# Routed experts with the weights standing still: a ring of six expert tiles, gate and up left turned, biases as columns

## What is computed

```python
logits = x @ router_weight.T + router_bias
top_val, top_idx = jax.lax.top_k(logits, TOP_K)
router_scores = zeros.at[rows, top_idx].set(softmax(top_val))
gate_up = einsum('th,ehd->etd', x, gate_up_proj) + gate_up_proj_bias[:, None, :]
gate, up = gate_up[..., ::2], gate_up[..., 1::2]
gate = minimum(gate, 7.0)
up = clip(up, -7.0, 7.0)
glu = gate * sigmoid(gate * 1.702)
out = einsum('etd,edh->eth', (up + 1.0) * glu, down_proj) + down_proj_bias[:, None, :]
out = (out * router_scores.T[:, :, None]).sum(axis=0)
```

## Time and profile before

| | us |
|---|---|
| Three timed runs, median (lowest to highest) | 987.29 (986.53 to 988.27) |
| The profiled execution | 992.78 |
| Its span, first to last instruction | 991.0 |
| First gather to last store issued, in that span | 59.13 to 234.31 |

### The profile page before, as it was taken

One profiled execution on the slowest core, in us unless ns is written; L12 is line 12 of the kernel. 1 busy time (PEld: TensorE's weight loads), 2 busy tenths in 40 slices (PEclk: granted clock), 3 DMA queues, 4 the chain that ended last, 5 costly groups with the idle time before them and its releaser, 6 DMA issues. The chain is left out here.

```text
span 991.0 us, 17524 instructions
## 1 busy us (share of the span) xinstructions
PE 921.8 (93%) x5677; PEld 739.2 (75%) x5677; DVE 748.4 (76%) x2035; ACT 585.3 (59%) x1711; POOL 490.0 (49%) x409
## 2 busy tenths in 40 slices
PE   7999999998889988996889999999999999999988
PEld 6455656665768655664678899988999889999976
DVE  6764564433785778998899889789887898788785
ACT  1753444437435778864664766756766667766743
POOL 3265667652124223434666565475664755645650
PEclk9998999999999989997999999999999999999999
DMA  9725212214101200000020100101002010000201
GB/s 320 285 87 222 78 67 86 75 75 184 47 1 62 86 2 2 3 22 0 22 64 1 32 13 2 65 1 44 1 1 65 1 43 1 4 20 2 97 1 43
DMA packets 19657, 55.18 MB, mean 56 GB/s; under 512 B 3264, under 2 KB 9488, under 8 KB 19056
## 3 DMA queue, kind: packets, MB, share of 16 engines
q1 hardware_dynamic: 13968, 40.68, 11.4%
q0 software_dynamic: 4512, 12.33, 3.6%
q10 hardware_dynamic: 1088, 1.05, 0.3%
HBM read 45.78 MB, written 8.26 MB: 55 GB/s over the span
## 5 line engine op out<-in xcount | busy, mean ns | idle before, releaser
L2513 ACT ACTIVATE y<-bank,g_mx 128x256 f32<-128x256 f32 x256 | 117.2, 484 | 115.6 <-DVE g_mx L2696 115.6
L2797 POOL TENSOR_TENSOR y<-y,g_sm 128x1024 f32<-128x1024 f32 x64 | 119.9, 1893 | 25.3 <-DVE g_sm L2712 25.3
L2773 POOL TENSOR_TENSOR g_c<-arena 128x1024 fp32r<-128x1024 f32 x30 | 64.0, 2132 | 112.4 <-DVE arena L2617 112.4
L2386 PE MATMUL bank<-arena 128*128 128x256 f32 x512 | 116.3, 380 | 0.0
L2386 PEld LDWEIGHTS bank<-arena 128*128 128x128 f32 x512 | 94.9, 190 | 12.0 <-issue 0.2
L767 PE MATMUL bank<-arena 128*128 x188 | 90.0, 602 | 0.0
L2269 PE MATMUL bank<-cst,y 128*128 128x128 f32 x512 | 71.9, 274 | 10.9 <-POOL y L2797 6.3
L2696 DVE TENSOR_REDUCE g_mx<-bank 128x2 f32<-128x512 f32 x128 | 79.2, 675 | 0.2 <-PE bank L2386 0.2
L1105 DVE TENSOR_SCALAR arena<-bank 128x256 f32<-128x256 f32 x47 | 19.9, 423 | 76.5 <-PE bank L767 68.1
L2363 PE MATMUL bank<-g_qh,g_xs 128*128 128x256 f32 x256 | 66.8, 298 | 7.0 <-POOL g_xs L2747 6.8
L2305 PE MATMUL bank<-g_ph,g_c 128*128 128x256 f32 x248 | 65.9, 304 | 4.0 <-ACT y L2513 2.3
(11 more groups left out here) (427 smaller groups left out, 2656.2 us busy)
## 6 DMA issues: line engine op xcount, KB each, us to landing
arena<-in_dram SPq DMA_DIRECT2D x16, 768.0 KB, 15.4
arena<-in_dram SPq DMA_DIRECT2D x21, 512.0 KB, 3.7
arena<-b_pairs SPq DMA_DIRECT2D x8, 512.0 KB, 7.4
arena<-in_dram SPq DMA_DIRECT2D x3, 1024.0 KB, 5.0
arena<-in_dram SPq DMA_DIRECT2D x2, 704.0 KB, 5.6
x<-in_dram SPq DMA_DIRECT2D x4, 256.0 KB, 5.1
cx<-in_dram SPq DMA_DIRECT2D x4, 256.0 KB, 5.3
cxT<-in_dram SPq DMA_DIRECT2D x4, 256.0 KB, 5.8
```

What stands on the lines that cost most here:

```text
L2386: m = pe.matmul(o[:, st * 256:st * 256 + 256], g_t[:, c, st * P:st * P + P], keys, start=True, stop=True)
L2513: m = act.activation(g_p[:, c, st, :], o[:, st * 256:st * 256 + 256], ACT.Exp, bias=g_mx[j % 2][:, 2 * c + st:2 * c + st + 1], accum_out=g ...
L2773: pool.tensor_tensor(cat, g_o[j % 2], g_om, ALU.subtract).then_inc(s_gc, 1)
L2797: pool.tensor_tensor(pf, pf, sums, ALU.mult).then_inc(s_gp, 1)
```

## The change

**Weights.** They are no longer held for all experts. A ring of six places (`NW`) takes the weights tile by tile: for each of the 47 tiles SP loads the expert's number from `b_et` into a register and issues one transfer of 768 KB, also where two tiles in a row have the same expert. From the seventh on it first waits until PE has done `down` of the tile six before. The first waits for `b_et` (`s_bet`). The next layer's two matrices are issued behind the sixth.

**Gate and up.** The weights now stand, in blocks of 128 by 128, and the turned rows stream, 128 columns at a time: eight products instead of two. Their result is the turned one, hidden width on the partitions, so `hidden_T` on PE and its copy on ACT are gone, and `down` waits for DVE's product alone. PE has no `value_load` left.

**Biases.** The product with the one-hot column is gone from the loop. Before it, four small products make a table of columns, `b_bt`, and DVE copies it out (`tile_bias_dve`). DVE then adds the bias while it clips, in four instructions of 128 columns instead of two of 256, and the lower clip of up moves into the multiplication. `bias_dve`, seven instructions that laid out the old table, is gone, and one of the two loads of the biases.

**Order ahead of the loop.** `experts_dve` now runs before `scores_dve` and the index table.

```diff
+        NW = 6
+        b_w = [arena[:, W_EXP * n:W_EXP * n + W_EXP] for n in range(NW)]
...
-        W_GROUPS = (range(0, 4), range(4, 8), range(8, W_LOW), range(W_LOW, NE))
-        s_bw = [sem(f"experts_loaded{g}") for g in range(4)]
+        s_bw = [sem(f"expert_of_tile_loaded{n}") for n in range(NW)]
...
+        plan(("B", "bt"), 7)
...
-            plan(("B", "hT", j), 4)
...
-            for g in range(3):
-                for e in W_GROUPS[g]:
-                    sp.dma_start(arena[:, W_AT[e]:W_AT[e] + W_EXP], ew_d[e]).then_inc(s_bw[g], 16)
-            D_first_sp(sp)
-            sp.wait_ge(s_bs, 2)
-            take(sp, ("B", "bd", 3))
-            for e in W_GROUPS[3]:
-                sp.dma_start(arena[:, W_AT[e]:W_AT[e] + W_EXP], ew_d[e]).then_inc(s_bw[3], 16)
+            sp.wait_ge(s_bet, 1)
+            for j in range(NTL):
+                if j >= NW:
+                    take(sp, ("B", "dn", j - NW))
+                e = sp.value_load(b_et[0:1, j:j + 1], min_val=0, max_val=NE - 1)
+                sp.dma_start(b_w[j % NW], ew_d[bass.ds(e, 1), :, :].rearrange("o p w -> (o p) w")).then_inc(s_bw[j % NW], 16)
+                if j == NW - 1:
+                    D_first_sp(sp)
...
             table(range(0, 4))
             K_raw_pe(pe, 11)
             table(range(4, T))
+            o = claim(pe, ("B", "bt"))
+            pe.wait_ge(s_bet, 1)
+            for m_ in range(4):
+                m = pe.matmul(o[:, m_ * NTP:m_ * NTP + NTP], b_raw[0:NE, m_ * P:m_ * P + P], b_sel[0:NE, :],
+                              start=True, stop=True)
+            fill(m, ("B", "bt"))
             for n in range(12, 14):
                 K_raw_pe(pe, n)
             route()
...
                     m = pe.transpose(o[:, k * P:k * P + P], b_xg[j % NR][:, k * P:k * P + P], ident)
                 fill(m, ("B", "xT", j))
...
 
-            def gate_up(j, at_):
+            def gate_up(j):
                 o = claim(pe, ("B", "gu", j))
-                pe.matmul(o[:, :], b_sel[:, j:j + 1].to_broadcast([P, P]), b_bias[:, :], start=True, stop=False)
+                pe.wait_ge(s_bw[j % NW], 16 * (j // NW + 1))
                 have(pe, ("B", "xT", j))
-                for k in range(KD):
-                    m = pe.matmul(o[:, :], b_xT[j % 2][:, k, :], arena[:, bass.ds(at_ + 512 * k, 512)],
-                                  start=False, stop=(k == KD - 1))
+                for m_ in range(4):
+                    for k in range(KD):
+                        c0 = 512 * k + m_ * P
+                        m = pe.matmul(o[:, m_ * P:m_ * P + P], b_w[j % NW][:, c0:c0 + P], b_xT[j % 2][:, k, :],
+                                      start=(k == 0), stop=(k == KD - 1))
                 fill(m, ("B", "gu", j))
 
-            def hidden_T(j):
-                o = claim(pe, ("B", "hT", j))
+            def down(j):
+                o = claim(pe, ("B", "dn", j))
                 pe.wait_ge(s_bh, j + 1)
                 for k in range(KD):
-                    m = pe.transpose(o[:, k * P:k * P + P], b_u2[j % 2][:, k * P:k * P + P], ident)
-                fill(m, ("B", "hT", j))
-
-            def down(j, at_):
-                o = claim(pe, ("B", "dn", j))
-                have(pe, ("B", "hT", j))
-                for k in range(KD):
-                    m = pe.matmul(o[:, 0:D], b_hT[j % 2][:, k, :], arena[:, bass.ds(at_ + 1024 + D * k, D)],
+                    c0 = 1024 + D * k
+                    m = pe.matmul(o[:, 0:D], b_hT[j % 2][:, k, :], b_w[j % NW][:, c0:c0 + D],
                                   start=(k == 0), stop=(k == KD - 1))
                 fill(m, ("B", "dn", j))
 
-            pe.wait_ge(s_bet, 2)
-            expert = {}
             rows_T(0)
             K_raw_pe(pe, NK - 1)
             for s_ in range(NTL + 2):
                 if s_ + 1 < NTL:
                     rows_T(s_ + 1)
                 if s_ < NTL:
-                    expert[s_] = pe.value_load(b_et[0:1, s_:s_ + 1], min_val=0, max_val=W_AT[NE - 1])
-                    if s_ < NE:
-                        for g in range(4):
-                            if s_ == W_GROUPS[g][0]:
-                                pe.wait_ge(s_bw[g], 16 * len(W_GROUPS[g]))
-                    gate_up(s_, expert[s_])
+                    gate_up(s_)
                 if s_ in (0, 1):
                     down_bias(2 * s_)
                     down_bias(2 * s_ + 1)
-                if 1 <= s_ <= NTL:
-                    hidden_T(s_ - 1)
                 if s_ >= 2:
-                    down(s_ - 2, expert[s_ - 2])
+                    down(s_ - 2)
             for n in range(NK):
                 K_tr_pe(pe, n)
 
...
                 o = take(act, ("B", "xT", j))
                 empty(act.copy(b_xT[j % 2], o[:, 0:2 * P].rearrange("p (k n) -> p k n", k=KD)), ("B", "xT", j))
 
-            def hidden_T(j):
-                if j >= 2:
-                    take(act, ("B", "dn", j - 2))
-                o = take(act, ("B", "hT", j))
-                empty(act.copy(b_hT[j % 2], o[:, 0:2 * P].rearrange("p (k n) -> p k n", k=KD)), ("B", "hT", j))
-
             def gelu(j):
                 act.wait_ge(s_bgt, j + 1)
                 act.activation(b_g[j % 2], b_g[j % 2], ACT.Gelu_apprx_sigmoid).then_inc(s_bt, 1)
...
             for s_ in range(NTL + 2):
                 if s_ + 1 < NTL:
                     rows_T(s_ + 1)
-                if 1 <= s_ <= NTL:
-                    hidden_T(s_ - 1)
                 if s_ < NTL:
                     gelu(s_)
                 if s_ >= 2:
...
             V.do(dve.tensor_scalar(b_ef, b_ef, float(NE - 1), None, ALU.min))
             V.sync()
             V.do(dve.tensor_scalar(b_sel[:, :], b_ef, const("lane"), None, ALU.is_equal))
-            V.do(dve.tensor_scalar(b_e2, b_ef, float(W_LOW), float(W_AT[W_LOW] - W_LOW * W_EXP), ALU.is_ge, ALU.mult))
-            V.sync()
-            dve.scalar_tensor_tensor(out=b_et, in0=b_ef, scalar=float(W_EXP), in1=b_e2, op0=ALU.mult, op1=ALU.add)\
-                .then_inc(s_bet, 1)
+            V.do(dve.tensor_copy(b_et, b_ef))
+            V.sync()
+            dve.tensor_copy(b_n[:, 0:1], b_ef[:, 0:1]).then_inc(s_bet, 1)
+
+        def tile_bias_dve(dve, V):
+
+            o = take(dve, ("B", "bt"))
+            bias = o[:, 0:4 * NTP].rearrange("p (m j) -> p m j", m=4)
+            V.do(dve.tensor_copy(b_bt[:, 0:2, :], bias[:, 0:2, :]))
+            empty(dve.tensor_scalar(b_bt[:, 2:4, :], bias[:, 2:4, :], 1.0, None, ALU.add), ("B", "bt"))
+            have(dve, ("B", "bt"))
+            V.sync()
 
         def slot_scores_dve(dve, V):
             dve.wait_ge(s_byst, 16 * B)
...
             V.do(dve.memset(b_z[:, :], 0.0))
             V.do(dve.memset(b_S[:, 0:1], 0.0))
             V.do(dve.memset(b_C[:, 0:1], 0.0))
-            bias_dve(dve, V)
             setup_dve(dve, V)
             mask_dve(dve, V)
             dve.wait_ge(s_bc, 16)
             V.do(dve.tensor_scalar(b_sp, const("iota")[:, 0:NTP], float(P), const("spare"), ALU.mult, ALU.add))
             place_dve(dve, V)
+            experts_dve(dve, V)
             scores_dve(dve, V)
             o = take(dve, ("B", "table"))
             V.sync()
...
             have(dve, ("B", "table"))
             dve.tensor_scalar(b_idx, b_dst, TOPK * B * S - 1, 2, ALU.bitwise_and, ALU.logical_shift_right)\
                 .then_inc(s_bidx, 1)
-            experts_dve(dve, V)
+            tile_bias_dve(dve, V)
             dve.wait_ge(s_byst, 16 * B)
             for c in range(2):
                 o = take(dve, ("B", "sT", c))
...
 
             def gate_up(j):
                 o = take(dve, ("B", "gu", j))
-                dve.tensor_scalar(b_g[j % 2], o[:, 0:D], 7.0, None, ALU.min).then_inc(s_bgt, 1)
-                if j >= 2:
-                    take(dve, ("B", "hT", j - 2))
-                empty(dve.tensor_scalar(b_u2[j % 2], o[:, D:2 * D], 8.0, -6.0, ALU.min, ALU.max), ("B", "gu", j))
+                for k in range(KD):
+                    m = dve.tensor_scalar(b_g[j % 2][:, k * P:k * P + P], o[:, k * P:k * P + P], b_bt[:, k, j:j + 1], 7.0,
+                                          ALU.add, ALU.min)
+                m.then_inc(s_bgt, 1)
+                for k in range(KD):
+                    m = dve.tensor_scalar(b_u2[j % 2][:, k * P:k * P + P], o[:, D + k * P:D + k * P + P],
+                                          b_bt[:, KD + k, j:j + 1], 8.0, ALU.add, ALU.min)
+                empty(m, ("B", "gu", j))
 
             def hidden(j):
                 have(dve, ("B", "gu", j))
                 dve.wait_ge(s_bt, j + 1)
-                dve.tensor_tensor(b_u2[j % 2], b_u2[j % 2], b_g[j % 2], ALU.mult).then_inc(s_bh, 1)
+                if j >= 2:
+                    take(dve, ("B", "dn", j - 2))
+                dve.scalar_tensor_tensor(out=b_hT[j % 2].rearrange("p k n -> p (k n)"), in0=b_u2[j % 2], scalar=-6.0,
+                                         in1=b_g[j % 2], op0=ALU.max, op1=ALU.mult).then_inc(s_bh, 1)
 
```

29 lines of the change are left out of this document (7 added, 22 removed).

## The result

The changed kernel takes 979.56 us (median of 4 runs, 979.02 to 981.63) against 987.78 (986.53 to 988.54) for the kernel before, measured beside it: a ratio of 0.9915, 95% interval 0.9894 to 0.9936. So it is 8.2 us faster, where 19 us were forecast (968.2). The direction and the length of a step were right, and the time lies in the range, in the part that the forecast gave to its first rival. The size of the gain was missed by more than half.

The account below looks back on a forecast made before the run. PE was taken to bound the loop. Loop -17.8, ahead of it +0.5, after it -1.8 sum to -19.1 us: 992.78 becomes 973.7 profiled, less 5.5 gives a median of 968.2 us, range 962 to 983.

Parts of the forecast that it names:

- first rival: Loop: GpSimd sets the step, 3.05 to 3.25 us; at 3.13 the time is 976.8; chance 0.24.
- Ahead of the loop: Before tile 3: later indices and gather, shorter first steps, the clock falling again; together +0.5 us.
- The loop: Tile 3 to tile 46: PE's step 2.93 us with waits, 43 steps 126.0 us against 143.76, -17.8 us.
- That one lies 5.5 above the median: Whole kernel: profiled execution 5.5 us above the timed median, so profiled 973.7 gives a median of 968.2.
- into DMA queues already full of weights: Ahead of the loop: indices and first gather 2.1 to 2.2 us later; full queues may add 0 to 2 us.
- 0.02 a step for waits that remain: Loop: PE waits left after DVE's product wait goes, added to a step of 2.91 us.
- is below 2.91 by 0.06 only: Loop: GpSimd's work, 2.85 us a step, just fits PE's 2.91; working four tiles ahead forgives a late start, not a longer step.
- signs of being wrong: Loop: PE waits for a DMA, GpSimd busy while PE idles, pass over 0.13 us; or clock below 1.00 beyond the first steps.
- After the loop: Gate and up of tile 46 to the last store: 5.1 us instead of 6.89, -1.8 us.
- fourth rival: Loop: weight loads not hidden, a step 4.12 us, time 1019; chance 0.03.
- The weights' way round: Loop: weights issued 8.9 us before they are wanted land in 5 to 8 us, 7 taken, so they fit.
- second rival: Loop: slower than before because weights return late, deciding from 8.9 us on, 1011 at 12 us; chance 0.07.

Follow-up runs that it names:

- second profile: The kernel before, unchanged, profiled again: 985.86 us, against 992.78 in the execution from which the forecast was made.
- both edits ahead of the loop and six buffers: Changed kernel, places before experts list, third and fourth down biases a step later, six finished-row buffers: 969.92 us; with GpSimd's subtractions behind its last store too: 966.37.
- the run with the subtractions behind the loop: Changed kernel with GpSimd's twelve subtractions for stage D moved from the loop to behind its last store: 975.38 us, ratio 0.9869.

## Why the forecast missed

Forecast and profile, from the books above, in the forecast's own terms:

```
                                        forecast   measured   miss
tile 3 starts at ("Ahead of the loop")     84.2      88.6      +4.4
tile 3 to tile 46 ("The loop")            126.0     126.75     +0.8
tile 46 to first combine                   12.1      14.4      +2.3
the rest                                  749.7     747.45     -2.2
outside the span                            1.8       1.8       0.0
profiled time                             973.7     979.0      +5.3
profiled time to median                    -5.5      +0.5      +6.0
median                                    968.2     979.6     +11.4
```

**"That one lies 5.5 above the median"** is the step that cost most, 6.0 us. The 5.5 us were treated as a constant lying on every profile. The second profile shows where such a distance comes from: between the two executions of one kernel it is the clock's fall in the first steps, 3.1 us, and 3.3 us more of waiting in the loop. How much of each the median run has is not known. The forecast had already taken the loop's share away by replacing 143.76 us with 43 clean steps, and the 5.5 us took it away again. It had kept the clock's fall for the new kernel, and the 5.5 us took that off as well. From the second profile, whose loop is 140.49 us, the loop's gain by the forecast's own 126.0 is 14.5 us and not 17.8.

**"Ahead of the loop"** was mis-sized, +0.5 against +4.95 (+8.0 on the second profile). The mechanism stood in the text: indices 2.1 us later, "into DMA queues already full of weights", with "0 to 2 us" for it. The first gather was issued at 61.12, as forecast (61.3), but its rows landed 7.8 us later. The forecast had 0.7 us of PE's margin used up and no wait; there was one of 3.24. The clock then fell twice. The loads were costed as something that the steps wait for, which they never did. What they did to the transfer among them was an estimate from no row. Nearest was the 768 KB landing time, 15.4 us with eleven queued, which should have made the upper end. The run with indices first shows the price of the order as a whole: with it undone tile 0 is back at 67.18. The two gathers behind the first then land in 2.8 us.

**The loop** came out within 0.8 us, by two misses that nearly cancel. A step is 2.871, not 2.91: sixteen passes take 1.79 us (150.46 to 152.25), 0.112 a pass, between the forecast's bounds of 0.107 and 0.119 and under the 0.114 taken. "0.02 a step for waits that remain" was 0.08 (3.3 us in 43 steps). The sentence on GpSimd named the cause and let it go: 2.85 us a step "is below 2.91 by 0.06 only", and a late start is forgiven. A lead of four tiles forgives a debt once, not six times. With the store at 1.29 us for tens of us, the work is (5 x 2.86 + 2) / 5 = 3.3 us a step there and the debt grows. The first rival, GpSimd setting the step, was thus the true one in kind. It cost 3.3 us instead of 8.6, because only part of the loop runs at that pitch and the lead absorbs the rest. Two of the forecast's own signs of being wrong came with it: PE waits for a gather in the loop (0.5 us, once), and GpSimd is busy without waits while PE idles. That the total of the loop was so close is luck.

**After the loop** 5.1 us were forecast to the last store and 6.38 came. `down` of the last three tiles ran in one row (217.14), as forecast. But then GpSimd issues three stores at its own pitch of 1.27 us:

```profile
219.21 0.96 POOL L871 DMA_INDIRECT b_pairs<-arena  x1 [1.96 <-ACT arena L846]
220.47 0.97 POOL L871 DMA_INDIRECT b_pairs<-arena  x1 [0.30 <-issue]
221.74 0.96 POOL L871 DMA_INDIRECT b_pairs<-arena  x1 [0.31 <-issue]
```

A stage that ends on a queue's own pitch was costed by PE's end. The transfers back took another 1.0 us, 8.0 from the last store to the first combine against 6.97. In the other kernels the same code took 7.0 to 8.7 us; no run isolates why. Nor is the row "the rest" explained: it was 747.5 to 750.3 us in the fourteen profiles of this case, for the same program. It hides the miss above it: from gate and up of tile 46 to the end of the span are 763.6 us before and 761.8 in after, -1.7 where -1.8 was forecast, but by terms that cancel and not by the ones of the forecast.

**What held.** Weight loads of 195 ns are hidden at one pass every 0.112 us, so the fourth rival is refuted on this kernel: 752 loads over the whole array, 0.1 us of idle time before them. With it falls the rule of the Trainium skill ("TensorE: Matmul & The Clock Gate", Part 3, The mechanism) as the forecast quoted it. The same section also says that a load into the background weight buffer is pulled ahead of matmuls in flight; the overlap in this trace agrees with that, the buffer itself no row shows. The weights' way round took 6.8 us (forecast 5 to 8), and PE never waited for it, so the second rival is gone. VectorE never held PE back in the loop, though its four instructions of 128 columns cost more than taken: they repeat every 0.26 us, so from start to start the four are 1.04 us (110.69 to 111.73 in after) against 0.67 for the two of 256 (102.55 to 103.22 in before), +0.37 instead of +0.2.

## To carry over

When a step gets shorter, ask of every helper engine that works ahead how much it gains per step on the bound, and compare that with its occasional extra work: a lead of n tiles pays a debt once, and a gain of zero per step never pays it back. A wait that is relieved at its own place (here, more buffers) can move to the twin that the same late engine feeds. A profile's distance to the median is not a constant to carry over when it may lie in the stretch that the change replaces; profile the kernel twice, and do not take the same waits off twice. And small transfers that start a loop should be issued ahead of the bulk ones.

## What was not expected of the hardware

- A gather of 128 KB issued among six weight loads of 768 KB landed 7.8 us after its issue, against 6 in the loaded loop and 2.8 us with the loads left out.
- DMA engines at a share of 0.99 and 375 GB/s, together with a step of 2.871 us, did not slow TensorE: with the loads left out (share 0.25) the step was the same.
- GpSimd's store takes 0.99 us or 1.26 to 1.30 us, and stays at one of the two for many steps: in after 1.29 from 115 to 140 us, 0.99 near 150. In the run with the subtractions behind the loop the gathers took 1.27 instead, from 107 to 139 us, and the stores 0.99. In both stretches store to store is 2.86 to 2.87 us, the step itself, and in the second profile of the kernel before no store in the loop takes over 1.15 us. So it may be a matter of what another engine does at that instant; no run here varied that, and it stays open. The Trainium skill ("GPSIMD Engine Reference", section 1, Specifications) says that GpSimd shares its SBUF interfaces with VectorE, with contention where VectorE's instruction has two SBUF inputs or runs in a mode that uses two ports.
- The granted clock fell behind gaps of PE of 1.0 to 3.2 us ahead of the loop in some executions and not in others: the kernel before had the same gap of 1.44 us in both profiles, and 0.77 or 1.00 in the stretch around it. Where PE had no gap (the two runs with both edits ahead of the loop and six buffers) it stayed at 1.00. What decides it no run shows.
